# Q of the last two token blocks by seven half products in place of eight, in a gated cross-attention and linear kernel on one core

## The reference

```python
Q = (layernorm(x) @ Wq.T).reshape(b, s, 8, 4, 128)
K = (ctx @ Wk.T).reshape(b, s, 8, 128)
V = (ctx @ Wv.T).reshape(b, s, 8, 128)
probs = softmax(where(causal, einsum(Q, K) * 128 ** -0.5, min))
x = x + tanh(g_xattn) * (einsum(probs, V).reshape(b, s, 4096) @ Wd.T)
x = x + tanh(g_ffn) * (layernorm(x) @ dequantize(qweight).T + bias)
```

## Time and profile before

| what | us |
|---|---|
| median of 3 runs | 1063.35 (1062.31 to 1066.21) |
| the profiled execution | 1062.54 |
| its span, first to last instruction | 1060.6 |
| PE busy | 1019.3 |
| DVE busy | 685.5 |
| ACT busy | 456.7 |
| POOL busy | 235.5 |

### The profile page before, as it was taken

One profiled execution on the slowest core, in us unless ns is written; L12 is line 12 of the kernel. 1 busy time (PEld: TensorE's weight loads), 2 busy tenths in 40 slices (PEclk: granted clock), 3 DMA queues, 4 the chain that ended last, 5 costly groups with the idle time before them and its releaser, 6 DMA issues.

```text
span 1060.6 us, 19976 instructions
## 1 busy us (share of the span) xinstructions
PE 1019.3 (96%) x7842; PEld 569.6 (54%) x7842; DVE 685.5 (65%) x1374; ACT 456.7 (43%) x917; POOL 235.5 (22%) x245
## 2 busy tenths in 40 slices
PE   4889999999998999999999999999999999999995
PEld 2455555555554555555555555555555555555542
DVE  5856677777578665765466556665556664555678
ACT  5777676676532343233334332244433323333322
POOL 1355565565604000210001200210000400000013
PEclk9999999999999999999999999999999999999998
DMA  7648655445355432444313643234333443223111
GB/s 276 217 155 286 209 163 186 160 132 158 103 176 200 96 87 96 159 130 136 107 56 112 198 138 122 78 121 120 126 117 118 131 136 115 62 96 134 69 37 60
DMA packets 90219, 142.61 MB, mean 134 GB/s; under 512 B 31248, under 2 KB 64016, under 8 KB 79504
## 3 DMA queue, kind: packets, MB, share of 16 engines
q1 hardware_dynamic: 90128, 141.34, 41.5%
HBM read 94.11 MB, written 25.17 MB: 112 GB/s over the span
## 4 chain that ended last, share of the span: by engine, by line
PE 86%; DVE 10%; ACT 2%; issue 2%; DMA 1%; SPq 0%; DVEq 0%; ACTq 0%
PE pa L1295 42%; PE py L1295 29%; PE av L1408 5%; PE pp L1391 3%; PE ps L1375 2%; PE py L1466 2%; PE pp L1375 2%; DVE q L897 1%; DVE wq L897 1%; DVE sc L943 1%; DVE row_max L941 1%; DVE sc L937 1%; DVE sc L954 1%; DVE xn L1053 1%; DMA xacc<-in_x 1%
## 5 line engine op out<-in xcount | busy, mean ns | idle before, releaser
L1295 PE MATMUL pa<-xT,wq 128*128 128x512 f16 x1536 | 344.4, 380 | 10.2 <-DVE q L897 7.5
L1295 PE MATMUL py<-wd,att 128*128 128x512 f16 x1488 | 336.2, 379 | 0.7 <-issue 0.7
L1295 PEld LDWEIGHTS pa<-xT,wq 128*128 128x128 f16 x1536 | 146.1, 98 | 192.0 <-issue 25.9
L1295 PEld LDWEIGHTS py<-wd,att 128*128 128x128 f16 x1488 | 143.2, 98 | 159.2 <-issue 1.1
L677 ACT ACTIVATE q<-pa 128x512 f16<-128x512 f32 x128 | 75.7, 591 | 264.8 <-PE pa L1295 264.8
L976 DVE SCALAR_TENSOR_TENSOR xacc<-py,f_y,xacc 128x512 f32<-128x512 f32 x128 | 95.7, 748 | 124.2 <-PE py L1295 124.2
L728 ACT ACTIVATE att<-av 128x256 f16<-128x256 f32 x256 | 80.8, 384 | 145.8 <-PE av L1408 145.3
L967 DVE SCALAR_TENSOR_TENSOR att<-av,att 128x256 f16<-128x256 f32 x256 | 93.5, 418 | 67.1 <-ACT att L728 66.9
L897 DVE SCALAR_TENSOR_TENSOR q<-pa,q 128x512 f16<-128x512 f32 x128 | 87.9, 686 | 58.7 <-ACT q L677 55.9
L1295 PE MATMUL pa<-wv,cT 128*128 128x128 f16 x1536 | 96.2, 219 | 0.0
L1295 PEld LDWEIGHTS pa<-wv,cT 128*128 128x128 f16 x1536 | 89.8, 98 | 0.9
(11 more groups left out here) (131 smaller groups left out, 1064.9 us busy)
## 6 DMA issues: line engine op xcount, KB each, us to landing
wq<-kept_q SPq DMA_DIRECT2D x24, 1024.0 KB, 7.1
wd<-kept_d SPq DMA_DIRECT2D x23, 1024.0 KB, 4.8
v_dup<-v_nat SPq DMA_DIRECT2D x128, 128.0 KB, 2.4
raw_d<-in_wdT SPq DMA_DIRECT2D x8, 1024.0 KB, 10.2
...
```

The lines of the kernel that those rows point to most:

```text
L1295: last = pe.matmul(out, stationary(a, i), moving(b, i), start=(i == 0 and (a, b) == PASSES[0]), stop=(i == count - 1 and (a, b) == PASSES[ ...
```

## The change

For m = 16 to 31 (blocks 2 and 3; the work is done in steps n = 15 to 30) Q is no longer four products of 512 contraction rows by 512 tokens. Two heads are taken as a pair r (0 or 1); weights and tokens are cut into 2 x 2 quarters (head of the pair x half of the 512 contraction rows, and that half x 256 tokens), and the four quarters of the result come from seven products of half size, numbered 1 to 7, with sums and differences of quarters as operands. Each is 2 chunks x 3 passes = 6 matmuls of 256 columns (`run(m, r, i)`).

Products 1, 6, 7, 4 add up one after another in one bank (X), 5 and 3 in a second (Y), 2 stands alone in a third (Z). Between the additions, ACT copies the bank: P1 (`copy_p1`), U2 = P1 + P6 (`copy_u2`), and P5 (`copy_p5`). DVE forms C11 = P1 + P2 (`add_11`), C22 = U2 + P7 + P5 (`add_22`), C12 = U2 + P5 + P3 (`add_12`); C21 is what bank X holds after product 4. ACT and DVE then write the high and low parts of each quarter. All of it stands in one sequence behind the scores of the step; the linear layer's units move behind it.

What the products need is made beforehand. Sums of Wq: in steps 13 to 20, one group each, SP loads the raw weights (`load_mix`), POOL makes four sums (`mix_weights`), ACT and DVE split them (`mix_hi`, `mix_lo`), SP stores them (`keep_mix`) and from step 22 loads them back (`back_mix`). Sums of the tokens: in steps 12 and 20 on POOL (`mix_norm`, `mixed_lo`) and ACT (`mixed_hi`); SP transposes them with 32 more DMAs a block, while xT itself needs 24 in place of 32. The norm of the next block comes one step earlier in blocks 1 and 2, the transposes stand in steps g = 4, 5, 6 (16, 20, 20), and `ffn_weight` moves to steps 9 and 10. Buffers are shared anew: `ws` and `tT` lie in the raw weight buffers, `u2` and `p5` in `junk`. `Q_SCALE` doubles and the squares of Wq are taken at twice the size, to leave room for the sums.

```diff
+            def run(m, r, i):
...
+                elif (r, i) == (1, 5):
+                    pe.wait_ge(c12_ok, pair_count(m, 0))
+                elif (r, i) == (1, 2):
+                    pe.wait_ge(c11_ok, pair_count(m, 0))
+                elif i == 6:
+                    pe.wait_ge(p1_ok, pair_count(m, r))
+                elif i == 7:
+                    pe.wait_ge(u2_ok, pair_count(m, r))
+                elif i == 3:
+                    pe.wait_ge(p5_ok, pair_count(m, r))
+                elif i == 4:
+                    pe.wait_ge(c22_ok, pair_count(m, r))
+                bank = (BANK_X if i in (1, 6, 7, 4) else BANK_Y if i in (5, 3) else BANK_Z)[r]
...
+                for kc in range(2):
+                    for c, d in PASSES:
...
+                        last = pe.matmul(half(bank), a[:, c, head, w_half + kc, :], b[:, d, b_half + kc, at],
...
@@ TensorE, step n
                 score_unit(n, 0)
                 score_unit(n, 1)
+                if fast(m):
+                    run(m, 0, 1)
+                    run(m, 0, 5)
+                    run(m, 0, 2)
+                    run(m, 0, 6)
+                    run(m, 0, 7)
+                    run(m, 0, 3)
+                    run(m, 1, 1)
+                    run(m, 0, 4)
+                    run(m, 1, 5)
+                    run(m, 1, 2)
+                    run(m, 1, 6)
+                    run(m, 1, 7)
+                    run(m, 1, 3)
+                    p_transpose(n, 0)
+                    run(m, 1, 4)
+                    if ffn is not None:
+                        ffn_unit(t0, n)
+                    k_unit(m)
...
@@ ScalarE, step n
+                if fast(m):
+                    copy_p1(m, 0)
+                    exp(n, 0)
+                    copy_p5(m, 0)
+                    copy_u2(m, 0)
+                    exp(n, 1)
+                    hi_11(m, 0)
+                    p_part(n, 0)
+                    p_part(n, 1)
+                    hi_22(m, 0)
+                    hi_12(m, 0)
+                    copy_p1(m, 1)
+                    hi_21(m, 0)
+                    copy_p5(m, 1)
+                    copy_u2(m, 1)
+                    hi_11(m, 1)
+                    hi_22(m, 1)
+                    hi_12(m, 1)
+                    p_transposed(n, 0)
+                    hi_21(m, 1)
+                    if mixing(n) is not None:
+                        mix_hi(mixing(n), (0, 1))
+                    k_part(m)
...
@@ VectorE
+            def add_22(m, r):
+
+                dve.wait_ge(r_mm, run_count(m, r, 7))
+                dve.wait_ge(p5_ok, pair_count(m, r))
+                dve.tensor_tensor(p5, half(BANK_X[r]), p5, ALU.add).then_inc(c22_ok, 1)
...
+                if fast(m):
+                    scores(n, 0)
+                    scores(n, 1)
+                    add_11(m, 0)
+                    normalise(n, 0)
+                    normalise(n, 1)
+                    p_part(n, 0)
+                    add_22(m, 0)
+                    add_12(m, 0)
+                    lo_11(m, 0)
+                    lo_22(m, 0)
+                    lo_12(m, 0)
+                    lo_21(m, 0)
+                    p_part(n, 1)
+                    add_11(m, 1)
+                    add_22(m, 1)
+                    add_12(m, 1)
...
-                    if n in (GROUPS, GROUPS + 1) and j % 2 == 1:
-                        ffn_weight(2 * (n - GROUPS) + j // 2)
+                    if n in (GROUPS + 1, GROUPS + 2) and j % 2 == 1:
+                        ffn_weight(2 * (n - GROUPS - 1) + j // 2)
@@ SyncE, step n
-                if dma_tiles(n) is not None:
-                    transpose_tiles(*dma_tiles(n))
+                if m + 1 >= FIRST_FAST + GROUPS and fast(m + 1):
+                    back_mix(m + 1)
+                transpose_first(n)
+                transpose_rest(n)
                 if m < STEPS:
                     duplicate_v(m)
                 if ffn_of(n) is not None:
                     for t in range(ffn_of(n) * TILES, (ffn_of(n) + 1) * TILES):
                         store(t)
+                if mixing(n) is not None:
+                    keep_mix(mixing(n))
+                if mixing(n + 1) is not None:
+                    load_mix(mixing(n + 1))
@@ GpSimd
+            def mix_weights(g):
+
+                pool.wait_ge(s_ld, 16 * (g + 1))
...
+                pool.tensor_tensor(a22, a22, a21, ALU.add).then_inc(s_mix, 1)
+                pool.tensor_tensor(a21, a11, a21, ALU.subtract).then_inc(s_mix, 1)
+                pool.wait_ge(s_mix, 4 * g + 2)
+                pool.tensor_tensor(a11, a22, a11, ALU.subtract).then_inc(s_mix, 1)
+                pool.wait_ge(s_mix, 4 * g + 3)
+                pool.tensor_tensor(a12, a12, a11, ALU.subtract).then_inc(s_mix, 1)
```

468 lines of the change are left out of this document (388 added, 80 removed).

## The result

The changed kernel takes 1118.3 us (median of 4 runs, 1117.6 to 1119.8) against 1063.2 us of the kernel before on the same chip: ratio 1.0515, 95% interval [1.0491, 1.0539]. It is 55 us slower. The profiled execution's span is 1114.9 us against 1060.6, 54.3 us more.

A forecast was written before the change was run, and what follows sets the result against it. PE, busy 96% of the span, bounds the kernel. From the profiled 1062.5 us, -23.0 + 22.7 + 24.8 + 2.2 + 7 + 4 + 3 + 2 - 4 + 4 = +42.7 gave 1105.2, forecast as 1106 us, range 1084 to 1128.

The forecast's parts named there:

- columns: Q in steps 15 to 30: 84 matmuls of 256 columns replace 48 of 512, 1.44 us saved a step; -23.0 us.
- U2: Product 7 waits for ACT's copy of the bank after product 6: 0.71 us, twice a step; +22.7 us.
- C22: The first pair's product 4 waits for VectorE's add_22, behind the softmax: 1.55 us in 16 steps; +24.8 us.
- VectorE late in steps 16, 24: VectorE first ends a norm's statistics there; the 1.11 us go straight into the wait for C22, twice; +2.2 us.
- POOL and VectorE collide: Steps 15 to 20: POOL's weight sums slow VectorE's normalisation, two collisions of 0.57 us a step; +7 us.
- transposes, step 15: Transposing DMAs bunched in SP's queue in steps 12 to 14 make step 15's product 1 wait; +4 us.
- step 20, late copies: ACT's mix_hi stands ahead of k_part and waits for a POOL sum whose load came late; +3 us.
- step 9: Moving ffn_weight one step on removes VectorE's lateness, PE's wait and the half clock there; -4 us.
- lower clock: Waits of some 3 us bring a lower clock: 2.5 stretches of 1.6 us, in steps 15, 20 and others; +4 us.
- rival 3: The columns give nothing, as small matmuls aren't in proportion (126 ns each): 1129 us; 3 in 100.
- Rival 1: VectorE's chain to add_22 is covered, so only the U2 wait is left: 1072 us, or 1064; 7 in 100.
- Rival 4: POOL and VectorE collide five times a step (+10), lower clock (+8), late transposes (+5): 1129 us; 10 in 100.

The follow-up runs named there:

- e11: The kernel before with one edit, ffn_weight one step later (steps 9 and 10 in place of 8 and 9); 1057.4 us, ratio 0.9961.
- e4: The changed kernel with POOL's four sums of the weights cut to one column of 256 in each; 1113.7 us, ratio 1.0482.
- e6: The changed kernel with seven extra 512-column matmuls before the first pair's product 4 in steps 15 to 20, 24 and 25; 1114.8 us, ratio 1.0498.
- e7: The changed kernel with all preparation kept, but Q of blocks 2 and 3 made by the old four products; 1067.7 us, ratio 1.0048.

## Why the prediction was right, and where its sizes were off

Forecast was 1106 us in a range of 1084 to 1128, slower with 0.92; measured 1118.3. Sign, mechanism and range were right. By terms, forecast and then measured in the profiled execution, in us:

| term | forecast | measured | from |
|---|---|---|---|
| columns | -23.0 | -22.4 | 14 x 0.656 a step |
| U2 | +22.7 | +19.8 | 32 x 0.62 |
| C22 | +24.8 | +23.7 | 16 x 1.48 |
| VectorE late in steps 16, 24 | +2.2 | +3.1 | idle above plain; part of step 16's is POOL's |
| POOL and VectorE collide | +7 | +8.1 | idle above plain, steps 17 to 20, 25 |
| transposes, step 15 | +4 | +5.3 | idle above plain |
| step 20, late copies | +3 | +2.4 | pT wait |
| steps 12 to 14 | +2 | +3.3 | step lengths |
| step 9 | -4 | -4.0 | step length, e11 |
| lower clock | +4 | +13.1 | busy above plain |

The terms measured give 52.4 us; step 26 adds 0.7, the start of the run 1.7 and its end -1.1, which makes 53.7 against 54.3 us between the spans.

**Columns, U2, C22: right.** They are worked out from single rows and came within 3 us each. The plain changed step was forecast at 31.8 us and is 31.64. U2's 0.71 us was 0.09 too long. The trace doesn't agree with the rule of the Trainium skill (TensorE: Matmul & The Clock Gate, Back-to-back issue gap) that the prediction weighed as rival 3: 0.656 / 6 = 109 ns a matmul of 256 columns in the changed step itself, 220 ns at 512, in proportion. Rival 1 has its answer as well. The chain to C22 was not covered in this order.

**The collisions: right in sum, wrong in place.** I put two collisions of 0.57 us into each of six steps and blamed POOL's sums of weights; that the sum agrees is luck. A single collision of the softmax costs up to 1.06 us. (The trace before had a longer one too: the 256-column form of the line in the earlier trace rows goes up to 1.13 us, 0.71 above its plain 0.42, at 48.88 us; the 0.57 was that of the 512-column form.) They sat in steps 17 to 20 and in step 25, where no weights are mixed. In step 25, in the first half of step 17 and in step 20 the partner is an addition of the linear layer (L710, in step 20 L716), POOL work that the kernel before had too. Step 18 in e4 is the proof for the sums; for the older work it is what e4 leaves in step 17, and step 20, where the wait for C22 is 3.43 us with the sums and 3.42 without. Late starts weigh in too: part of step 20's excess is VectorE starting its scores 1.3 us later than in a plain step, for which I had no term.

**The late start of step 16: only in part the cause that I gave.** I had a start 1.11 us late, from the norm's statistics, and put it into C22. In step 16 VectorE's scores start 3.75 us after the step (568.27), in step 24 1.98 us. The 1.77 us between the two are two operations of 8 columns that ran beside POOL's sums of weights (L679 and L680, from 565.71 to 568.21):

```profile
566.12 0.89 DVE L1166 TENSOR_SCALAR f_score<-w_prod,c_both 128x8 f32<-128x8 f32 x1
566.92 1.31 DVE L1168 TENSOR_SCALAR f_y<-w_prod,c_both 128x8 f32<-128x8 f32 x1
```

In e4, without those sums, they take 0.21 and 0.23 us. So this too is POOL's doing, which I had left out of this step. It came out as a wait for U2, since on ACT copy_u2 stands behind the exponential of the small half, which a late VectorE delays (PE, step 16):

```profile
570.87 1.42 PE L1742 MATMUL pa<-raw_q,raw_d 128*128 128x256 f16 x6 [2.27 <-ACT junk L916]
```

Where no sums are in the way the late start goes into C22 as forecast: step 16 of e4 waits 0.47 us for U2 and 2.45 for C22, and step 24 of the changed kernel 2.45 too, against 1.33 plain, and 1.11 more were forecast.

The Trainium skill (SBUF — State Buffer, Who interferes with whom) says that the two engines hold the shared port in turn and the second waits fully. The row of step 17 agrees in kind: an operation of 0.42 us took 1.48 us, 1.06 more, which is under one whole POOL addition (1.45 us). Not every operation was hit, so the 33 us estimated by that rule did not come.

**The lower clock: the term that failed.** The step of the prediction was "waits of that size I expect in step 15, in step 20 and in one or two where the C22 chain meets POOL: 2.5 x 1.6". The price of 1.6 us a stretch was right (steps 18 and 24 lost 1.6 and 1.4), the count was not: 13.1 us are about eight stretches. It came from one row, a wait of 2.98 us, and I read it as if only waits of 3 us counted. Waits of 2.27 to 2.45 us were followed by it too:

```profile
642.70 1.46 PE L1742 MATMUL pa<-raw_q,wq 128*128 128x256 f16 x6 [2.30 <-DVE junk L1211]
...
642.70:646.20 3.50, 3.50 (x18) 2.45 (x19) 2.30 (x6) 1.74 (x5) 0.00 (x0) 0.52 0.14 17
```

So most waits of over 2 us were paid about twice, once idle and once at 1.2 GHz; not the one of 3.56 us in step 17. With eight stretches in the term the sum would have been 1115. Rival 4 had this as one of its parts ("the lower clock follows most long waits"), at 8 us and with the whole rival at 10 in 100; the other two parts stayed near the forecast. The 1.33 us waits of the plain steps had the full clock behind them in all of steps 21 to 23 and 27 to 29.

**Step 9: right,** and e11 shows it by itself.

What stays open: what makes the chip grant the lower clock behind one wait of 2.0 us and not behind another of 3.6, or of the same 2.0 in the same step (step 26 of the changed kernel and of e6). A difference of 2 or 3 us between two profiles can be this alone. And the 0.7 us in step 13 that e7 doesn't have (31.85 against 31.2) was not looked into.
